# Transposes ahead of scores, lo parts ahead of the row maximum, in each attention step of a two-layer kernel

## The reference, cut to what matters

```python
hn = group_norm(x, gn1_scale, gn1_bias)
qkv = einsum('bchw,oc->bohw', hn, w_qkv) + b_qkv      # 8 heads of q, k, v
wgt = softmax(einsum('bct,bcs->bts', q * scale, k * scale), axis=-1)
a = einsum('bts,bcs->bct', wgt, v)
out = group_norm(einsum('bchw,oc->bohw', a, w_proj) + b_proj, gn2_scale, gn2_bias)
x = x + out
```

## Time and profile before

| | |
|---|---|
| median of the runs | 3531.57 us |
| the profiled execution | 3531.65 us, of which the span is 3529.9 us |
| PE busy | 98% of the span |
| DVE busy | 59% |
| ACT busy | 52% |
| POOL busy | 31% |
| mean granted clock of PE | 0.998 |

### The profile page before, as it was taken

One profiled execution on the slowest core, in us unless ns is written; L12 is line 12 of the kernel. 1 busy time (PEld: TensorE's weight loads), 2 busy tenths in 40 slices (PEclk: granted clock), 3 DMA queues, 4 the chain that ended last, 5 costly groups with the idle time before them and its releaser, 6 DMA issues.

```text
span 3529.9 us, 52658 instructions
## 1 busy us (share of the span) xinstructions
PE 3460.3 (98%) x17360; PEld 2834.5 (80%) x17360; DVE 2079.4 (59%) x3388; ACT 1825.5 (52%) x3074; POOL 1083.4 (31%) x947
## 2 busy tenths in 40 slices
PE   7999999999999999999999999999999999999999
PEld 3788788888888788887888878788787887888878
DVE  4577446774367733786347854478544784447742
ACT  3577226772268622785227842378323882248822
POOL 1244212442034410454104531045211452114521
PEclk9999999999999999999999999999999999999999
DMA  7622215222143123341133311342203422143210
GB/s 267 186 49 61 108 37 143 51 59 95 54 127 87 34 84 86 95 96 72 36 109 86 82 72 43 114 96 61 84 37 108 96 61 84 38 129 74 60 48 24
DMA packets 63519, 294.41 MB, mean 83 GB/s; under 512 B 9200, under 2 KB 9456, under 8 KB 52464
## 3 DMA queue, kind: packets, MB, share of 16 engines
q1 hardware_dynamic: 63216, 290.65, 27.9%
HBM read 158.49 MB, written 31.46 MB: 54 GB/s over the span
## 4 chain that ended last, share of the span: by engine, by line
PE 86%; issue 6%; DVE 3%; ACT 2%; DMA 2%; POOL 1%; SPq 0%; ACTq 0%; DVEq 0%; POOLq 0%
PE big L432 28%; PE tps L532 14%; PE big L559 12%; PE ops L545 12%; PE ops L705 10%; PE big L629 6%; PE ops L432 1%; ACT PB L831 1%; DMA d_m<-PT 1%; DMA d_u<-ST 1%; PE big L597 1%; DVE XA L1254 1%; POOL XA L972 1%; PE big L460 0%; DVE HL L1259 0%
## 5 line engine op out<-in xcount | busy, mean ns | idle before, releaser
L962 POOL TENSOR_SCALAR PB<-PB,small 128x1024 f32<-128x1024 f32 x576 | 648.0, 1125 | 1305.4 <-DVE small L1188 1294.6
L837 ACT ACTIVATE PT<-tps 128x512 fp32r<-128x512 f32 x1088 | 601.0, 596 | 251.7 <-PE tps L532 248.7
L1193 DVE TENSOR_TENSOR PT<-tps,PT 128x512 fp32r<-128x512 f32 x1088 | 692.8, 678 | 39.0 <-ACT PT L837 38.6
L1182 DVE TENSOR_REDUCE small<-big 128x1 f32<-128x1024 f32 x512 | 624.8, 1220 | 67.5 <-PE big L559 64.3
L532 PEld LDWEIGHTS tps<-ident,PB 128*128 128x128 f32 x4608 | 527.0, 140 | 124.9 <-DVE PT L1193 56.0
L532 PE MATMUL tps<-ident,PB 128*128 128x128 f32 x4608 | 617.8, 275 | 8.9 <-DVE PT L1193 6.1
L831 ACT ACTIVATE PB<-big,small 128x1024 f32<-128x1024 f32 x512 | 572.1, 1117 | 76.5 <-DVE small L1182 73.5
L545 PE MATMUL ops<-PT,VT 128*128 128x512 f32 x2048 | 599.0, 414 | 0.0
L559 PE MATMUL big<-ST 128*128 128x512 f32 x2048 | 556.0, 393 | 13.7 <-ACT PB L831 11.2
L559 PEld LDWEIGHTS big<-ST 128*128 128x128 f32 x2048 | 382.4, 188 | 105.0 <-ACT PB L831 19.7
L545 PEld LDWEIGHTS ops<-PT,VT 128*128 128x128 f32 x2048 | 346.1, 189 | 47.1 <-DVE PT L1193 5.0
(11 more groups left out here) (157 smaller groups left out, 4655.2 us busy)
## 6 DMA issues: line engine op xcount, KB each, us to landing
ST<-ST SPq DMA_DIRECT2D x384, 256.0 KB, 5.0
W<-d_qk SPq DMA_DIRECT2D x32, 1024.0 KB, 5.2
XA<-in_x SPq DMA_DIRECT2D x8, 2048.0 KB, 7.7
X<-in_x SPq DMA_DIRECT2D x8, 2048.0 KB, 10.4
W<-d_wp SPq DMA_DIRECT2D x8, 2048.0 KB, 11.7
W<-d_g SPq DMA_DIRECT2D x8, 2048.0 KB, 11.9
W<-d_m SPq DMA_DIRECT2D x8, 2048.0 KB, 7.8
W<-d_u SPq DMA_DIRECT2D x8, 2048.0 KB, 10.2
```

Of the source, the lines that this page charges most:

```text
L837: act_fn(pt_slot(u, s)[:, 0, :], tps[n % 2][:], ACT.Copy).then_inc(s_pt_hi, 1)
L962: nc.gpsimd.tensor_scalar(PB[:, i, :], PB[:, i, :], rinv[:, i:i + 1], 1.0, ALU.mult, ALU.mult)\
L1182: V.tensor_reduce(negmax[:, i:i + 1], tile(("s", 4 * u + tb))[:], axis=AX.X, op=ALU.max, negate=True).then_inc(s_row_max, 1)
L1193: V.tensor_tensor(pt_slot(u, s)[:, 1, :], tps[n % 2][:], pt_slot(u, s)[:, 0, :].bitcast(f32), ALU.subtract).then_inc(s_pt_ready, 1)
```

## The change

On PE the two calls of `transposes` move ahead of `scores0` and `project_last_v`. On DVE the two calls of `pt_lo` move ahead of `row_max`, `last_v_lo` and the `recip` of a unit's later steps. ACT's, POOL's and SP's programs stay. No instruction and no wait is added or removed.

```diff
                     if qk_part(step) is not None:
                         project_qk(qk_part(step))
+                    if n >= 0:
+                        transposes(n // 8, n % 8)
+                        transposes(n // 8, n % 8 + 1)
                     if step < STEPS0:
                         scores0(u, tb)
                     if last_values(step):
                         project_last_v(last_values(step))
-                    if n >= 0:
-                        transposes(n // 8, n % 8)
-                        transposes(n // 8, n % 8 + 1)
                     if n > 0:
                         values0(n - 2)
                         values0(n - 1)
...
                     if tb == 0 and 4 <= step <= STEPS0:
                         recip((step - 1) // 4, (step - 1) % 4)
+                    if n >= 0:
+                        pt_lo(n // 8, n % 8)
+                        pt_lo(n // 8, n % 8 + 1)
                     if step < STEPS0:
                         row_max(u, tb)
                     if last_values(step - 1):
                         last_v_lo(last_values(step - 1))
                     if 1 <= step < STEPS0 and tb:
                         recip((step - 1) // 4, (step - 1) % 4)
-                    if n >= 0:
-                        pt_lo(n // 8, n % 8)
-                        pt_lo(n // 8, n % 8 + 1)
```

## The result

The changed kernel takes 4073.61 us, the median of 4 runs from 4069.78 to 4079.07, against 3532.05 for the kernel before: 1.1534 times as long, with a 95% interval of 1.152 to 1.1549. The forecast was 4050, between 4010 and 4150.

The account below looks back on a forecast made before the run. PE was taken as the bound (98% busy, 86% of the chain); the change closes an ACT-DVE ring, 252.8 against 189.2 us a batch, 64.8 with step 5, 518 for eight batches: 3532 + 518 = 4050 us, range 4010 to 4150.

Parts of the forecast that it names:

- The ring: Layer 0's attention, ACT and DVE: exponential, `pt_hi`, `pt_lo` x2, row maximum, next exponential; 4.16 us a plain step against PE's 2.71; chance 0.78.
- projection steps: Layer 0 attention steps with a q/k projection, 11 of 58 intervals: put at 4.93 us each, below PE's 5.45.
- each `a_hi`: ACT's half of `HH` between an exponential and the next `pt_hi`, six times from step 47: 0.52 each, 3.1 us a batch.
- the stage: Layer 0's attention from the exponential of step 5 to that of step 63: 252.8 us a batch against 189.2.
- The distances: Four start-to-start times in a plain step: 0.62 to lo parts, 1.19 to row maximum, 1.25 to exponential, 1.10 to ACT's next.
- the far end: Upper bound: lo parts at their whole 1.29 and a second such handover, 0.2 a step, 93 us; 4189 with PE-set q/k steps.
- PE setting the projection steps: Layer 0's q/k steps at PE's 5.45 instead of 4.93: 5.7 us a batch, 46 in all, counted only in the range.
- Finds no taker: Claim that PE's earlier transposes bring nothing: done 1.8 us before ACT wants them, as ACT is still in its exponential.
- The tail: Steps 64 to 68 of a batch: claimed to keep their work in an order the change does not touch in effect.
- PE's share: Sign expected in the changed kernel's profile: PE's share falls to about 85%, its transposes waiting for the lo parts.
- The rival of the low clock: Pauses of some 1.4 us in plain steps lower PE's clock; decides from mean granted clock 0.65; 4524 us; chance 0.08.
- No slower: ACT and DVE keep up with PE: 3509 us, or 3532 if the edit closes no ring; chance 0.02 for both.

## Why the prediction was right

**The ring.** It is there as put, and the size holds: 4.18 against 4.16 in plain steps, 4.93 against 4.93 in projection steps, and 0.52 for each `a_hi`, 253.8 against 252.8 us for the stage. The kernels that take something out of the ring carry the cause: a lo part out of it gives 0.60 a step, a shorter maximum 0.53, and one step of distance for the exponential opens it.

**The bound.** The distances came out at the sum itself and at neither of its ends: the waiting receiver starts as soon in the ring as in the rows of before, and of the 0.2 a step at the far end 0.02 came. PE setting the projection steps (46 us) did not come either.

**PE's part.** "Finds no taker" is the sentence that failed. In plain steps it is so, but in projection steps the transposes would stand in the ring without this move, 100 us in all. That the sum stayed right is luck on this point: its 4.93 counted on transposes that are ready, without my seeing that it took the move to make them so.

**What the sum left out.** The forecast of 518 us was 23 short of the 540.6. The stage's growth was 520 and not 509 (0.02 a step more, and 3.5 us in the last batch). The tail was put at nothing ("an order that the change does not touch in effect"), and that failed: PE, now early, does step 64's work ahead of time and then waits 2.4 us for POOL's `normalise`; behind that its clock falls in six of the eight batches, and each of the six pays 1.2 us. Layer 1's clock fell in five batches where it fell in one before, some 6 us; no run shows that the change is the cause. One sign missed as well: PE's share is 89% and not 85%, since the same matmuls are booked with more time (3.1 us a plain step and not 2.71).

**The rival of the low clock.** It is not what happens in the steps. From 700 to 880 us, where PE pauses ahead of the transposes of most steps, the granted clock is

```profile
700.00:880.00 180.00, 144.80 (x744) 107.89 (x742) 107.86 (x173) 109.34 (x198) 70.59 (x61) 1.00 0.20 47
```

1.00, far above the 0.65 from which it would decide. The rule of the Trainium skill that stood on that side ("TensorE: Matmul & The Clock Gate", section "A second HAM failure mode: psum-queue depth-cycling") does not come true for these pauses, most of 0.9 to 1.6 us.

The stretch also holds one pause of 2.44 us, ahead of the first transposes of a unit, and the clock stays up behind it. In the third batch it falls behind the same pause:

```profile
732.55 1.09 PE L532 MATMUL tps<-ident,PB 128*128 128x128 f32 x8 [2.44 <-POOL PB L962]
...
1229.11 1.09 PE L532 MATMUL tps<-ident,PB 128*128 128x128 f32 x8 [2.43 <-POOL PB L962]
...
732.55:736.55 4.00, 4.00 (x25) 3.25 (x26) 2.24 (x4) 2.18 (x4) 1.27 (x1) 1.00 0.71 148
1229.11:1233.11 4.00, 4.00 (x16) 3.33 (x17) 2.24 (x4) 2.18 (x4) 1.26 (x1) 0.63 0.69 145
```

The clock falls there in two batches of the eight (the third and the seventh), and it costs nothing: the stage of these two takes 253.8 us as in the second batch, since PE is not in the ring. What costs is a clock that falls in the tail and in layer 1, where PE sets the pace.

**No slower.** The rival asked for a ring under 2.71; it is 4.18. A ring of the hi and lo parts without maximum and exponential, which is what the kernel before has, leaves PE the bound.

## What to carry to other kernels

Where two engines hand work to each other twice in a step, write down the order of each list and follow one item round: if a step's first result on one engine stands behind the other's second in its list, the lists form a ring, its length is the sum of the start-to-start distances, and no engine's busy share warns of it. A move that only brings work forward can close such a ring, and each half of a paired move has to be followed by itself: here either half alone costs as much as both or more. When a bound moves from one engine to a ring, look for what the old bound's engine now does early and then waits for, since it can lose its clock there.

## What the runs showed of the hardware

**A pause of one length, two outcomes.** Layer 1 has a pause of PE of 1.83 us in each batch, in code that the change does not touch. These are the first matmuls behind it in two batches of the changed kernel, and the windows:

```profile
436.94 0.50 PE L629 MATMUL big<-HH,W 128*128 128x512 f32 x1 [1.83 <-DVE HL L1259]
...
438.20 1.02 PE L629 MATMUL big<-HH,W 128*128 128x512 f32 x2
...
935.01 0.50 PE L629 MATMUL big<-HH,W 128*128 128x512 f32 x1 [1.83 <-DVE HL L1259]
...
936.27 0.63 PE L629 MATMUL big<-HH,W 128*128 128x512 f32 x2
...
437.00:441.00 4.00, 4.00 (x12) 3.20 (x13) 3.09 (x2) 0.00 (x0) 4.00 (x2) 0.65 0.18 17
935.00:939.00 4.00, 3.99 (x17) 3.30 (x18) 3.15 (x2) 0.00 (x0) 4.00 (x2) 1.00 0.15 18
```

In one batch the clock falls and the stage takes some 1.6 us longer, in the other it stays up. By the granted clock in the 4 us behind this pause it fell in one of the eight batches of the kernel before, in five of the changed kernel, and in seven of the kernel with both moves in the projection steps alone. In that last kernel it makes about 10 us: from a batch's last exponential to the next batch's first takes 227.6 to 228.1 each time, where the kernel before has 226.0 to 226.5 in all but one.

The tail's pause does the same. In the changed kernel's third batch it has the length of the second batch's, and the clock stays at 1.00 where that had 0.60:

```profile
1384.70 1.09 PE L532 MATMUL tps<-ident,PB 128*128 128x128 f32 x8 [2.37 <-POOL PB L962]
...
1384.70:1388.70 4.00, 3.94 (x24) 2.98 (x24) 2.07 (x5) 2.30 (x5) 1.27 (x1) 1.00 0.00 0
```

In all, the clock fell behind the tail's pause in six batches of eight, and behind the steps' pause of 2.44 us in two. What decides it is not shown here; none of the runs changed only when the pause comes.

**A slower handover in the last batch.** The last batch's code stands outside the loop over batches. There the exponential starts 1.31 behind the row maximum instead of 1.25:

```profile
3706.70 1.22 DVE L1182 TENSOR_REDUCE small<-big 128x1 f32<-128x1024 f32 x1
3708.01 1.11 ACT L831 ACTIVATE PB<-big,small 128x1024 f32<-128x1024 f32 x1 [1.44 <-DVE small L1182]
```

In a ring that is 3.5 us over the batch (58 x 0.06). Why this handover takes longer there stays open.
